# Feed-forward of 32 units in six groups of 6, 5, 5, 5, 5 and 6 instead of four groups of eight

## The reference, cut to what matters

```python
# x: (8, 256, 1024); weight: 16 adapters of 1024 x 1024; up: (16, 64, 256); down: (16, 256, 64)
y = einsum('bsi,boi->bso', x, weight[ids])     # an adapter's matrix for each of the 8 sequences
t = y.reshape(2048, 1024)[:, perm].reshape(2048, 16, 64)
t = einsum('bhd,hdm->bhm', t, up)              # 16 heads, 64 -> 256
t = gelu(t, approximate=False)
t = einsum('bhm,hmd->bhd', t, down)            # 256 -> 64
out = x + t.reshape(2048, 1024)[:, argsort(perm)]
```

## Time and profile before

| | us |
|---|---|
| median of 3 runs (lowest, highest) | 290.91 (290.67, 291.04) |
| the profiled execution | 290.89 |
| its span (first to last instruction) | 289.1 |
| TensorE busy | 282.8 |
| VectorE busy | 196.2 |
| ScalarE busy | 161.7 |
| first product, until the first up matmul | 185.1 |
| each of the four groups of the feed-forward | 25.0 |
| from the last matmul to the end of the span | 3.9 |

### The profile page before, as it was taken

The page is one execution under the profiler, slowest core; times in us unless marked ns, Lnnn a source line. Parts: engine busy times, 40 slices in busy tenths (PEclk is TensorE's granted clock), DMA queues, the critical chain, the costliest instruction groups (busy, mean ns, idle before and its releaser), DMA issues.

```text
span 289.1 us, 4401 instructions
## 1 busy us (share of the span) xinstructions
PE 282.8 (98%) x1694; PEld 215.8 (75%) x1694; DVE 196.2 (68%) x227; ACT 161.7 (56%) x179; POOL 103.3 (36%) x96
## 2 busy tenths in 40 slices
PE   6999999999999999999999999999999999999994
PEld 6889898898898898898998998983376358338531
DVE  3688777767857949969859857562953675395333
ACT  5657328228237237456355350299579939948920
POOL 2000000008777000981000245175677773362054
PEclk9999999999999999999999999999999999999998
DMA  6999999889999999899977496665357743132033
GB/s 204 356 390 408 381 337 373 309 334 339 403 418 406 415 413 403 294 355 392 413 302 260 141 309 188 223 202 166 147 167 205 209 184 145 65 120 109 2 145 145
DMA packets 23796, 77.88 MB, mean 269 GB/s; under 512 B 2784, under 2 KB 11360, under 8 KB 18912
## 3 DMA queue, kind: packets, MB, share of 16 engines
q1 hardware_dynamic: 7056, 43.39, 39.0%
q0 software_dynamic: 7584, 25.18, 25.1%
q10 hardware_dynamic: 9136, 9.05, 9.0%
HBM read 60.82 MB, written 16.78 MB: 268 GB/s over the span
## 4 chain that ended last, share of the span: by engine, by line
PE 96%; DMA 1%; POOL 1%; SPq 1%; issue 0%; DVE 0%; ACT 0%; POOLq 0%; DVEq 0%
PE ps L588 38%; PE ps L598 20%; PE ps L650 19%; PE ps L626 5%; PE ps L629 5%; PE ps L632 5%; PE ps L564 3%; PE ps L569 1%; DMA w_raw<-w 1%; POOL out_rows L288 1%; SPq L200 1%; DVE w_raw L486 0%; ACT w_hi L380 0%; POOLq L308 0%; SPq L228 0%
## 5 line engine op out<-in xcount | busy, mean ns | idle before, releaser
L588 PE MATMUL ps<-x_pair,w_hi 128*128 128x512 f32 x480 | 111.7, 390 | 0.0
L588 PEld LDWEIGHTS ps<-x_pair,w_hi 128*128 128x128 f32 x480 | 89.2, 188 | 17.9
L332 ACT ACTIVATE w_hi<-w_raw 128x1024 fp32r<-128x1024 f32 x58 | 58.0, 1049 | 37.4 <-PE ps L588 22.1
L270 POOL DMA_INDIRECT t_raw<-y_rows,idx x32 | 40.8, 1274 | 97.1 <-DMA y_rows<-y_out 81.7
L443 DVE TENSOR_TENSOR w_lo<-w_raw,w_hi 128x1024 fp32r<-128x1024 f32 x60 | 70.5, 1216 | 0.8 <-PE ps L569 0.8
L472 DVE TENSOR_REDUCE y_out<-ps 128x256 f32<-128x512 f32 x64 | 42.3, 686 | 36.0 <-PE ps L598 36.0
L598 PEld LDWEIGHTS ps<-x_pair,w_lo 128*128 128x128 f32 x480 | 59.6, 192 | 1.2
L598 PE MATMUL ps<-x_pair,w_lo 128*128 128x256 f32 x480 | 59.9, 283 | 0.0
L361 ACT ACTIVATE hidden<-ps 128x1024 f32<-128x1024 f32 x48 | 46.9, 1024 | 18.1 <-PE ps L632 16.4
L650 PE MATMUL ps<-hidden,down_sb 128*64 128x512 f32 (+1 forms) x264 | 55.8, 581 | 0.0
L650 PEld LDWEIGHTS ps<-hidden,down_sb 128*64 128x64 f32 x264 | 18.6, 137 | 35.5 <-issue 29.4
(11 more groups left out here) (29 smaller groups left out, 155.3 us busy)
## 6 DMA issues: line engine op xcount, KB each, us to landing
w_raw<-w SPq DMA_DIRECT2D x29, 1024.0 KB, 7.8
y_rows<-y_out ACTq DMA_DIRECT2D x32, 256.0 KB, 6.4
x_raw<-x_cols SPq DMA_DIRECT2D x7, 1024.0 KB, 8.1
w_raw<-w SPq DMA_DIRECT2D x4, 256.0 KB, 4.6
w_raw<-w SPq DMA_DIRECT2D x2, 512.0 KB, 7.6
t_raw<-up SPq DMA_DIRECT2D x1, 1024.0 KB, 8.0
down_sb<-down SPq DMA_DIRECT2D x1, 1024.0 KB, 11.8
w_raw<-w SPq DMA_DIRECT2D x2, 384.0 KB, 6.4
```

The source lines that it names most:

```text
L270: nc.gpsimd.indirect_dma_start(t_raw[:, f % TG, :], None, y_rows[0:D * (chunk + 1), :], rows_of(f)).then_inc(t_in[f % TG], 16)
L332: nc.scalar.activation(w_hi[:, g % WS, k, :], w_raw[:, g % WRAW, k, :], ACT.Copy).then_inc(w_hi_done, 1)
L588: last = nc.tensor.matmul(y_bank(g, o), w_hi[:, ws, k, col], x_pair[:, xs, k, :, :], start=(k == 0), stop=False)
```

## The change

The groups get the sizes 6, 5, 5, 5, 5, 6. A group of six has 12 halves, of which 2, 5 and 8 are copied; a group of five has 10, of which 2 and 5 are copied. ScalarE's order is given by `ORDER`. The first bank of a group's down units is still `ps0`, whose last half is 8 in both sizes (0, 4, 8 lie in it): copied by VectorE in a group of six, read by ScalarE's GELU in a group of five. `hidden` has places for six units in place of eight. Ahead of the feed-forward six units are split in place of eight. The `t_low` of the next group stand one behind the second `add_x`, and two behind each later one.

```diff
-GROUP = 8
+SIZES = (6, 5, 5, 5, 5, 6)
+FROM = [sum(SIZES[:j]) for j in range(GROUPS + 1)]
-COPIED = (2, 5, 8, 11)
+COPIED = {6: (2, 5, 8), 5: (2, 5)}
+ORDER = {6: (0, 1, 3, 4, 6, 7, 9, 2, 10, 5, 11, 8), 5: (0, 1, 3, 4, 6, 7, 2, 8, 5, 9)}
+        def last_half(j, bank):
+            return max(h for h in range(MT * SIZES[j]) if h % BANKS == bank)
...
             for j in range(GROUPS):
-                gelu(j, 0)
...
+                for h in ORDER[SIZES[j]]:
+                    if h in COPIED[SIZES[j]]:
+                        gelu_in_place(j, h)
+                    else:
+                        gelu(j, h)
...
+                ahead = list(range(FROM[j + 1], FROM[min(j + 2, GROUPS)]))
+                for i in range(SIZES[j]):
+                    add_x(FROM[j] + i)
+
+                    for f in ahead[0:0 if i == 0 else 1 if i == 1 else 2]:
+                        t_low(f)
+                    ahead = ahead[0 if i == 0 else 1 if i == 1 else 2:]
...
-                        pe.wait_ge(added, GROUP * (j - 1) + 2 * (h + 1))
+                        if 2 * h < SIZES[j - 1]:
+                            pe.wait_ge(added, FROM[j - 1] + min(2 * (h + 1), SIZES[j - 1]))
+                        else:
+                            up_banks_free(j - 1, last_half(j - 1, h))
...
                 if i % 2 == 0:
-                    up_banks_free(j, PARTS - BANKS + i // 2)
+                    up_banks_free(j, last_half(j, i // 2))
```

More of the change, by code:

```diff
@@ L50 @@
 WRAW, WS, XS = 4, 2, 2
-YS, TG, SS, HS, XR = 4, 16, 8, 8, 10
+YS, TG, SS, HS, XR = 4, 16, 8, 6, 10
 PAIR, BANKS = 2, 4
-GROUP = 8
-GROUPS = NF // GROUP
-PARTS = GROUP * MT
-COPIED = (2, 5, 8, 11)
-GELU_PLACE = {0: 0, 1: 1, 3: 2, 4: 3, 6: 4, 7: 5, 9: 6, 10: 7, 12: 8, 2: 9, 13: 10, 5: 11, 14: 12, 15: 13, 8: 14, 11: 15}
+SIZES = (6, 5, 5, 5, 5, 6)
+GROUPS = len(SIZES)
+FROM = [sum(SIZES[:j]) for j in range(GROUPS + 1)]
+COPIED = {6: (2, 5, 8), 5: (2, 5)}
+ORDER = {6: (0, 1, 3, 4, 6, 7, 9, 2, 10, 5, 11, 8), 5: (0, 1, 3, 4, 6, 7, 2, 8, 5, 9)}
 UP_UNITS = (16, 17)
@@ L174, in up_banks, with group_of @@
             return ps[h % BANKS]
+        def group_of(f):
+            return next(j for j in range(GROUPS) if f < FROM[j + 1])
         def gelus_to(j, h):
-            return PARTS * j + GELU_PLACE[h] + 1
+            return MT * FROM[j] + ORDER[SIZES[j]].index(h) + 1
         def copies_to(j, h):
-            return len(COPIED) * j + COPIED.index(h) + 1
+            return sum(len(COPIED[n]) for n in SIZES[:j]) + COPIED[SIZES[j]].index(h) + 1
+        def last_half(j, bank):
+            return max(h for h in range(MT * SIZES[j]) if h % BANKS == bank)
         def token_parts(f):
@@ L190, in down_place @@
                 return ps[0][:, 0, 0:S]
-            return ps[f % GROUP // 2][:, f % 2, :][:, token_parts(f)[0]]
+            i = f - FROM[group_of(f)]
+            return ps[i // 2][:, i % 2, :][:, token_parts(f)[0]]
         def w_landed(g):
@@ L298, in _ @@
             for j in range(GROUPS):
-                for f in range(TG + GROUP * j, TG + GROUP * (j + 1)):
+                for f in range(TG + FROM[j], TG + FROM[j + 1]):
                     if f < NF:
                         gather_t(f)
-                for f in range(GROUP * j, GROUP * (j + 1)):
+                for f in range(FROM[j], FROM[j + 1]):
                     scatter(f)
@@ L358, in gelu @@
             def gelu(j, h):
-                act.wait_ge(up_done, PARTS * j + h + 1)
+                act.wait_ge(up_done, MT * FROM[j] + h + 1)
                 place = hidden[:, h // MT, h % MT, :, :]
@@ L409, in _ @@
                     up_high(UP_UNITS.index(g + 1))
-                if T_FROM <= g < NL - 2:
+                if T_FROM <= g < T_FROM + 2 * SIZES[0]:
                     t_high((g - T_FROM) // 2)
-            t_high(GROUP - 1)
             for j in range(GROUPS):
-                gelu(j, 0)
[L416 to L432, removed]
+                for h in ORDER[SIZES[j]]:
[3 more added lines that the diff above has]
+                        gelu(j, h)
+                    if j == 0 and h == 0:
+                        y_park(NL - 1)
                 if j + 1 < GROUPS:
-                    for f in range(GROUP * (j + 1), GROUP * (j + 2)):
+                    for f in range(FROM[j + 1], FROM[j + 2]):
                         t_high(f)
@@ L475, in up_copy @@
             def up_copy(j, h):
-                dve.wait_ge(up_done, PARTS * j + h + 1)
+                dve.wait_ge(up_done, MT * FROM[j] + h + 1)
                 nc.vector.tensor_copy(hidden[:, h // MT, h % MT, :, :], up_banks(h)[:, :, :]).then_inc(up_copied, 1)
@@ L519, in _ @@
                     up_low(UP_UNITS.index(g))
-                if T_FROM <= g < NL - 2 and g % 2 == 1:
+                if T_FROM <= g < T_FROM + 2 * SIZES[0] and g % 2 == 1:
                     t_low((g - T_FROM) // 2)
-                if g == NL - 2:
-                    t_low(GROUP - 1)
             for j in range(GROUPS):
-                for h in COPIED:
+                for h in COPIED[SIZES[j]]:
                     up_copy(j, h)
[L528 to L548, removed]
+                ahead = list(range(FROM[j + 1], FROM[min(j + 2, GROUPS)]))
[4 more added lines that the diff above has]
+                    ahead = ahead[0 if i == 0 else 1 if i == 1 else 2:]
         @block.tensor
@@ L601, in up_banks_free @@
             def up_banks_free(j, h):
-                if h in COPIED:
+                if h in COPIED[SIZES[j]]:
                     pe.wait_ge(up_copied, copies_to(j, h))
@@ L607, in up_unit @@
             def up_unit(f):
-                j, ts = f // GROUP, f % SS
+                j, ts = group_of(f), f % SS
                 if f == 0:
@@ L613, in up_unit @@
                     col = slice(m * P, (m + 1) * P)
-                    h = MT * (f % GROUP) + m
+                    h = MT * (f - FROM[j]) + m
                     if h >= BANKS:
@@ L635, in down_unit @@
             def down_unit(f):
-                j, i = f // GROUP, f % GROUP
+                j = group_of(f)
+                i = f - FROM[j]
                 if f == 0:
@@ L640, in down_unit @@
                 if i % 2 == 0:
-                    up_banks_free(j, PARTS - BANKS + i // 2)
+                    up_banks_free(j, last_half(j, i // 2))
                 for n, tok in enumerate(token_parts(f)):
                     if n == 1:
-                        pe.wait_ge(added, GROUP * j + 1)
+                        pe.wait_ge(added, FROM[j] + 1)
                     acc = down_place(f, n)
@@ L650, in down_unit @@
                             last = nc.tensor.matmul(acc[h * DH:(h + 1) * DH, :], down_sb[:, 2 * (f % FU) + h, m, :],
-                                                    hidden[:, f % HS, m, h, tok], start=(m == 0), stop=(m == MT - 1))
+                                                    hidden[:, i, m, h, tok], start=(m == 0), stop=(m == MT - 1))
                     last.then_inc(down_done, 1)
```

## The result

The changed kernel takes 299.47 us (median of 6 runs, 299.13 to 301.17), the kernel before 290.99 us beside it (6 runs). The ratio is 1.030, 95% interval 1.027 to 1.032: slower, by 8.5 us. The prediction said 299.4. The profiled execution took 299.25 us, its span is 297.4.

A forecast was written before the change was run, and what follows sets the result against it. TensorE was taken to bound the kernel, busy 282.8 of 289.1 us; 290.89 + 8.04 for four stops + 0.46 for two added turns = 299.39, forecast 299.4 us, 2.9% slower, range 297.9 to 302.4.

The forecast's parts named there:

- The stop: Ahead of down in each group of five, TensorE waits 2.01 us for ScalarE's GELU of half 8; four times, 8.04 us.
- the hand-off: From the end of ScalarE's GELU of half 8 to TensorE's first down matmul: taken as 0.12 us.
- The turns: TensorE going from down to up and back: 0.23 us each, two more with two more groups, 0.46 us.
- the down unit: One unit's down matmuls on TensorE: 13.88 / 8 = 1.735 us, read from a group of eight.
- The bound of 1.0 for both: Upper bound in us on the cost of the two added changes between down and up, forecast at 0.46.
- the passage: From the first product to the first group's up matmuls: TensorE has no gap there, so nothing to gain, 0.
- No stop at all: At the first down matmul of a group of five TensorE does not wait: 291.35 us, not slower; chance 0.04.
- a smaller loss: ScalarE reaches half 8 sooner than 0.92 and 0.95 us a GELU, total down to 293.6 us; chance 0.04.
- the likeliest case: TensorE's four waits ahead of down in groups of five come as worked out, clock staying full; chance 0.72.
- the rival: TensorE's clock falls to 1.2 GHz in the stops: 301 to 302.4 us for one or two, 305.4 for four; chance 0.17.
- The estimate of the price: One fall of TensorE's clock: a slow spell of an estimated 3 us, costing 1.5 us of work.
- The 1.15 us an activation: Trainium skill's estimate for ScalarE's 1024-element GELU: a stop of 3.3 us and 304.6 us in all; given no chance.

## Why the prediction was right

**The bound.** TensorE sets the end in both kernels, 96 and 92% of the chain. A loss of work on VectorE (two copies fewer, 196.2 to 193.4 us busy) brought nothing, as said. TensorE's busy time is 284.9 us and not near 283; about half of the rise is its 22 warm-up matmuls, which took 5.07 us in place of 4.10 with no effect on the first product's end.

**The stop.** Forecast 2.01 us in four groups, found 1.90, of which the profile shows 1.85 as idle: a group of five lasts 17.70 us (221.46 to 239.16) with the stop and 15.80 without it, in the kernel whose tiles go round. ScalarE's GELUs stood where the working put them, T + 6.92 and T + 7.86 against 6.94 and 7.89. What was too high is mostly the hand-off: 0.12 was taken from one case at the start, and the row here has 0.06. Sum 4 x 1.90 = 7.6 in place of 8.04.

**The turns.** Taken at 0.23 us each, they are dearer. From groups without a stop: 2 x 18.84 + 4 x 15.80 = 100.88 us for six groups, against 4 x 24.99 = 99.96 for four, so 0.92 us for two added turns, 0.46 each. The step that was too low is the down unit: 13.88 / 8 = 1.735 us spreads a part of the turn over the units. Eight units take 13.88 us and five take 221.46 - 212.72 = 8.74, so a unit is 5.14 / 3 = 1.713, and 0.17 us of the 13.88 belong to the turn beside the 0.23. The bound of 1.0 for both had held. The sum 7.6 + 0.92 = 8.5 us is what was measured; the forecast's 8.04 + 0.46 was the same sum with two errors of 0.4 and 0.5 against each other. That it met the median to 0.1 us is luck; that it lay within a microsecond isn't.

**What was put at nothing.** The first up matmul comes at 184.95 instead of 185.11, so the passage gave nothing but 0.16 us. The last add of a group starts at 221.87, 0.41 behind the group's end, and no half 2 waited. The first residual gather was issued at 206.21, near 206 as said. The groups of six had no stop.

**The rivals.** No stop at all and a smaller loss are out. The clock stayed at 2.4 GHz in the profile of the change through four stops of 1.85 us, so the likeliest case was the right one; but the rival is no empty one, since one stop of this length in another kernel brought a fall, and the change itself, when it ran again, had falls at its stops of 10.25 and 2.96 us. One of the six timed runs of the change (301.17 us) stands 1.8 us above the median of the others at a mean clock of 0.993 in place of 0.998 to 1.000; one fall would fit that, which no profile shows. The estimate of the price, 1.5 us, was near: 1.7. That is partly luck, for the rows that it was worked out from the earlier trace rows show the granted clock at 1.00 throughout and so no slow spell. The 1.15 us an activation that the prediction worked out and gave no chance is out as a duration too: the rows here have 1.02 to 1.07 us, and starts 0.91 to 0.94 apart. The page's rule that TensorE can swing between two clocks where it cycles through PSUM tiles with short idle spells between (the Trainium skill, TensorE: Matmul & The Clock Gate, A second HAM failure mode: psum-queue depth-cycling) agrees with the kernel with half 8 last, whose clock fell at each of its four stops and came back each time. The profile of the change shows no such swing.

## What to carry to other kernels

When two stages share a ring of buffers, changing a group's size changes which buffer the second stage meets first, and with it which item of the first stage it waits for. Work out that one item, its place in the slower engine's queue and its end against the moment when the bounding engine arrives; let the ring go on round instead of starting again at buffer 0, and the wait is gone, here for groups of five and six. A reordering in which every engine has nearly the same work can still cost 3%.

## What the runs showed of the hardware that I had not expected

Equal stops of TensorE need not cost the same: of ten of 1.85 to 2.00 us one was followed by some 3.4 us at 1.2 GHz (1.7 us lost) and nine by none, while those of 2.35, 2.96, 3.71 and 4.74 us all were followed by 3.4 or more. In four sets of five, ScalarE, VectorE and TensorE paused at once in one stretch; the cause is open. It cost the kernel before 12.2 us, 5.1 of them through a fall of TensorE's clock, and the version whose tiles go round 7 to 8 us without a fall.
